# A layer of attention and experts on one core: the order of the prologue, of the routing steps and of the last product

## The reference

```python
x = L0_attn_h                                   # (2, 1024, 256)
xn = _layernorm(x)
x = x + attn(xn) + ffn(xn)

def attn(h):                                    # 16 heads of 128
    z = layernorm(h) * ln_g + ln_b
    q, k, v = z @ wq.T + bq, z @ wk.T + bk, z @ wv.T + bv
    q, k = rope(q), rope(k)
    a = softmax(causal(q @ k.T / sqrt(128)))
    return (a @ v) @ wo.T + bo + h

def ffn(x):                                     # 2048 tokens, 32 experts
    scores = sigmoid(x @ gate_w.T)              # + bias; best 2 of 4 groups, then best 4 experts
    out = moe(x, topk_idx, topk_w * 2)          # at most 64 rows per expert, in token order
    shared = silu(x @ shared_gate) * (x @ shared_up) @ shared_down
    return out + shared
```

## Time and profile before

| | |
|---|---|
| time, median of 3 runs | 1031.75 us (1031.66 to 1031.94) |
| time of the profiled execution | 1031.76 us |
| span of the profiled execution, first to last instruction | 1029.5 us |
| busy: TensorE, VectorE, GpSimd, ScalarE | 1014.0, 717.4, 768.8, 664.8 us |
| chain that ended last: TensorE, VectorE, GpSimd | 91%, 4%, 2% |
| granted clock of TensorE, mean | 0.997 |
| granted clock from about 10.3 to 13.7 us | 0.53 in that stretch, behind an idle TensorE from 7.06 to 8.87 us |
| TensorE busy in 0 to 25, 25 to 50, 50 to 75, 75 to 100 us | 20.64, 24.39, 23.06, 23.54 us |
| TensorE busy in 1000 to 1029.5 us | 25.34 us |

### The profile page before, as it was taken

One profiled execution on the slowest core, in us unless ns is written; L12 is line 12 of the kernel. 1 busy time (PEld: TensorE's weight loads), 2 busy tenths in 40 slices (PEclk: granted clock), 3 DMA queues, 4 the chain that ended last, 5 costly groups with the idle time before them and its releaser, 6 DMA issues.

```text
span 1029.5 us, 18761 instructions
## 1 busy us (share of the span) xinstructions
PE 1014.0 (98%) x6461; PEld 906.7 (88%) x6461; DVE 717.4 (70%) x1746; ACT 664.8 (65%) x1454; POOL 768.8 (75%) x656
## 2 busy tenths in 40 slices
PE   8999999999999999999999999999999999999998
PEld 4788898899988898899989999899998989898997
DVE  8966777787787778766566666666666575665676
...
DMA packets 51677, 75.42 MB, mean 73 GB/s; under 512 B 12288, under 2 KB 29056, under 8 KB 51456
## 3 DMA queue, kind: packets, MB, share of 16 engines
...
...
## 4 chain that ended last, share of the span: by engine, by line
PE 91%; DVE 4%; POOL 2%; ACT 1%; DMA 1%; issue 0%; SPq 0%; DVEq 0%; POOLq 0%; ACTq 0%
PE ps L302 25%; PE ps L304 25%; PE ps L303 25%; PE ps L441 12%; PE ps L524 3%; PE ps L536 1%; DVE ps L1541 1%; POOL qb L1686 1%; POOL qb L1682 1%; POOL qs L1683 1%; DMA qs<-qb 0%; DMA ra_<-sh_gate 0%; ACT prob L1038 0%; DVE st L1232 0%; PE ps L510 0%
## 5 line engine op out<-in xcount | busy, mean ns | idle before, releaser
L1682 POOL TENSOR_TENSOR qb<-qb,k_sb 128x512 f32<-128x512 f32 x128 | 171.7, 1341 | 148.3 <-DMA qs<-qb 148.0
L1541 DVE CUSTOM_DVE_ANT_0 ps<-ps,maskr 128x128 f32<-128x128 f32 (+7 forms) x256 | 193.8, 762 | 58.3 <-PE ps L304 58.0
L1038 ACT ACTIVATE prob<-ps,nmax 128x128 f32<-128x128 f32 (+7 forms) x256 | 190.5, 744 | 61.6 <-DVE nmax L1541 59.8
L1049 ACT ACTIVATE ptd_h<-ps 128x128 fp32r<-128x128 f32 (+3 forms) x256 | 109.4, 436 | 152.2 <-PE ps L441 151.2
L1551 DVE TENSOR_TENSOR ptd_l<-ps,ptd_h 128x128 fp32r<-128x128 f32 (+3 forms) x256 | 124.4, 486 | 83.6 <-ACT ptd_h L1049 81.5
L1686 POOL TENSOR_TENSOR qb<-qb,qs 128x512 f32<-128x512 f32 x128 | 165.8, 1296 | 18.7 <-POOL qs L1683 0.4
L441 PE MATMUL ps<-k_sb,prob 128*128 128x128 f32 x1152 | 172.8, 274 | 3.4 <-DVE ol L1564 1.5
L1683 POOL TENSOR_TENSOR qs<-qs,k_sb 128x512 f32<-128x512 f32 x128 | 173.7, 1357 | 0.0
L441 PEld LDWEIGHTS ps<-k_sb,prob 128*128 128x128 f32 x1152 | 135.4, 141 | 20.6 <-issue 3.4
L302 PE MATMUL ps<-k_h,q_h 128*128 128x512 f32 (+3 forms) x384 | 140.2, 365 | 0.6 <-ACT ztmp L920 0.5
L1581 DVE SCALAR_TENSOR_TENSOR acc<-ps,rinv,acc 128x256 f32<-128x256 f32 x256 | 111.6, 478 | 32.5 <-PE ps L304 30.9
...
## 6 DMA issues: line engine op xcount, KB each, us to landing
qs<-qb SPq DMA_DIRECT2D x256, 128.0 KB, 2.3
...
```

The costliest lines, as they stand in the source:

```text
L1038: act.activation(prob[:, t % 2, 0:w], tile[t], ACT.Exp, bias=nmax[:, t:t + 1], scale=-1.0, accum_out=rsum[:, t:t + 1]).then_inc(exp_done, 1)
L1049: act.activation(turned(0, t, j0, w), src, ACT.Copy).then_inc(pth_done, 1)
L1541: dve.tensor_tensor_reduce(out=tile[t], in0=tile[t], in1=maskr[:, SEQ - w:SEQ], scale=-1.0, scalar=3e38, op0=ALU.add, op1=ALU.min, accum_o ...
L1682: pool.tensor_tensor(qb[:, i, :], qb[:, i, :], cos_sb[:, c], ALU.mult).then_inc(rope_a, 1)
```

## The change

The change moves instructions; it adds no arithmetic, apart from one VectorE operation and one DMA at the end. Its parts:

1. Prologue, first rows: `shared_lo_w(0)` and `shared_lo_w(1)` go from VectorE to GpSimd, each behind a `root_of` of group 0. On VectorE x_lo(0) stands ahead of first_root(1) and stats(1,0), stats(1,1) behind z_lo(0) and wqk_lo(0), stats(2,0) behind x_lo(1,0). On ScalarE both x_hi stand ahead of shared_w(1); wv_hi, shared_w(2) and wo_hi behind logits(0); shared_tanh(0,0) directly behind again(0). On TensorE shared(0,0,0) stands ahead of z's turns, with 17 and 8 dummies instead of 12 and 13, and shared(0,1,1) ahead of project(0,0).
2. Prologue, later: values(0,1) ahead of turn_x(2,1), values(0,2) ahead of down(1,0), down(3,0) ahead of scores(0,0).
3. Units: in unit 0 project(1,2) ahead of turn(0,2); masks(9,1) behind weighted and exps, masks(9,3) behind scores(9,7).
4. Routing: the pieces are dealt anew over units 9 to 12, and the DMA of the weights is waited for in unit 12, not 11.
5. End: the last `out_lo_part`, outproj, add_out and the output DMA are halved.

The diff, cut to what the text speaks of:

```diff
             pe.wait_ge(zeros_ready, 1)
-            idle(12)
+            idle(17)
             pe.wait_ge(id_in, 16)
             turn_tiles(xn, "xt", xn_tile, xn_ready)
-            idle(13)
+            idle(8)
+            shared(0, 0, 0)
             turn_tiles(zz, "zt", z_tile, z_ready)
             gate(0)
-            shared(0, 0, 0)
             shared(0, 0, 1)
             shared(0, 1, 0)
             turn_x(1, 0)
+            shared(0, 1, 1)
             project(0, 0)
-            shared(0, 1, 1)
             project(0, 1)
...
             shared(1, 0, 1)
+            values(0, 1)
             turn_x(2, 1)
             down(0, 0)
             shared(1, 1, 1)
-            values(0, 1)
...
             gate_turn(1)
+            values(0, 2)
             down(1, 0)
-            values(0, 2)
...
             gate_turn(3)
+            down(3, 0)
             scores(0, 0)
-            down(3, 0)
             down(3, 1)
...
                 scores(n, 3)
+                weighted(n - 1, 1, range(4))
                 masks(n, 1)
-                weighted(n - 1, 1, range(4))
+                if n == 0:
+                    project(n + 1, 2)
                 turn(n, 2)
                 weighted(n - 1, 1, range(4, 8))
                 expert_turn(n)
                 scores(n, 4)
-                project(n + 1, 2)
+                if n:
+                    project(n + 1, 2)
...
                 scores(n, 6)
-                masks(n, 3)
...
                 scores(n, 7)
+                masks(n, 3)
...
             shared_w(0)
             x_hi(0, 0)
+            x_hi(0, 1)
             shared_w(1)
-            wv_hi(act, 0)
-            x_hi(0, 1)
             gate_w()
             again(0)
+            shared_tanh(0, 0)
             affine(0, 0)
             affine(0, 1)
-            shared_w(2)
-            wqk_hi(act, 0)
-            wo_hi(act, 0)
             z_hi(0, 0)
             z_hi(0, 1)
-            shared_tanh(0, 0)
+            wqk_hi(act, 0)
             logits(0)
+            wv_hi(act, 0)
+            shared_w(2)
+            wo_hi(act, 0)
...
             stats(0, 0)
-            shared_lo_w(dve, 0)
             first_root(0)
             norm(0)
             stats(0, 1)
-            stats(1, 0)
-            first_root(1)
-            shared_lo_w(dve, 1)
             x_lo(0, 0)
             x_lo(0, 1)
+            first_root(1)
+            stats(1, 0)
             gate_w()
             biases_q()
+            shared_g(0, 0)
             norm(1)
+            z_lo(dve, 0, 0)
+            z_lo(dve, 0, 1)
+            wqk_lo(dve, 0)
             stats(1, 1)
...
+                elif n == MASKS and at == 1:
+                    route_chosen_scores()
                 elif n == MASKS and at == 2:
+                    route_scan(0)
+                elif n == MASKS + 1 and at == 0:
+                    route_scan(1)
+                elif n == MASKS + 1 and at == 1:
+                    route_want()
+                elif n == MASKS + 1 and at == 2:
                     route_sums()
-                elif n == MASKS + 1 and at == 1:
+                elif n == MASKS + 2 and at == 0:
+                    route_find(0)
+                elif n == MASKS + 2 and at == 1:
                     route_inverse()
-                elif n == MASKS + 1 and at == 2:
+                elif n == MASKS + 2 and at == 2:
                     route_weights()
-                elif n == MASKS + 1 and at == 0:
-                    route_scan(0)
-                elif n == MASKS + 2 and at == 0:
-                    route_scan(1)
-                elif n == MASKS + 2 and at == 2:
-                    route_find(0)
...
             root_of(0, 0, 1)
+            shared_lo_w(pool, 0)
             root_of(0, 1, 2)
+            shared_lo_w(pool, 1)
             root_of(1, 0, 3)
             wv_lo(pool, 0)
-            pool.wait_ge(swl_ready, 2)
             shared_lo_w(pool, 2)
```

More of the change, by code:

```diff
@@ L497, in outproj @@
                 for i in range(2):
+                    single = u == UNITS - 1 and c == i2 == 1
+                    if single:
+                        pe.wait_ge(ol_done, 2 * u + 3 + i)
+                        if i:
+                            bank = take("OQ", u)
                     t = slice((2 * i2 + i) * P, (2 * i2 + i + 1) * P)
@@ L816, in _ @@
             sp.dma_start(out_t[2], acc[:, 2 * GT:3 * GT, :]).then_inc(stored, 16)
-            for i in range(2):
-                sp.wait_ge(add_done, 4 * (UNITS - 1) + 3 + i)
-                t = slice(3 * GT + 2 * i, 3 * GT + 2 * i + 2)
-                sp.dma_start(out_t[3, :, 2 * i:2 * i + 2, :], acc[:, t, :]).then_inc(stored, 16)
-            sp.wait_ge(stored, 16 * 5)
+            for done, a, b in ((3, 0, 2), (4, 2, 3), (5, 3, 4)):
+                sp.wait_ge(add_done, 4 * (UNITS - 1) + done)
+                sp.dma_start(out_t[3, :, a:b, :], acc[:, 3 * GT + a:3 * GT + b, :]).then_inc(stored, 16)
+            sp.wait_ge(stored, 16 * 6)
         def rope_in(act, m, i):
@@ L1304, in _ @@
             stats(0, 1)
-            stats(1, 0)
-            first_root(1)
-            shared_lo_w(dve, 1)
             x_lo(0, 0)
             x_lo(0, 1)
+            first_root(1)
+            stats(1, 0)
             gate_w()
             biases_q()
+            shared_g(0, 0)
             norm(1)
+            z_lo(dve, 0, 0)
+            z_lo(dve, 0, 1)
+            wqk_lo(dve, 0)
             stats(1, 1)
-            wqk_lo(dve, 0)
-            z_lo(dve, 0, 0)
-            shared_g(0, 0)
-            z_lo(dve, 0, 1)
-            stats(2, 0)
+            shared_u(0, 0)
             shared_g(0, 1)
             x_lo(1, 0)
-            shared_u(0, 0)
+            stats(2, 0)
             shared_u(0, 1)
+            x_lo(1, 1)
             norm(2)
-            x_lo(1, 1)
             stats(2, 1)
@@ L1452, in route_scan, with route_want @@
                                                ALU.add, ALU.add))
+            def route_want():
+                stepped(dve.tensor_scalar(want[:, :], k_sb[:, C_CV:C_CV + CG], 1.0, None, ALU.add))
             def route_find(half):
                 j = slice(half * CG // 2, (half + 1) * CG // 2)
-                if half == 0:
-                    stepped(dve.tensor_scalar(want[:, :], k_sb[:, C_CV:C_CV + CG], 1.0, None, ALU.add))
                 stepped(dve.max_index(found[:, j], want[:, j], cum))
@@ L1567, in out_lo_part @@
                 dve.wait_ge(oh_done, 2 * u + 2 + h)
-                o = slice(2 * h * P, (2 * h + 2) * P)
-                dve.tensor_tensor(ol[1][:, o], rbank("PW" if h else "PV", u, 1)[:, o], oh[1][:, o].bitcast(F32),
-                                  ALU.subtract).then_inc(ol_done, 1)
+                for o in (slice(2 * P, 3 * P), slice(3 * P, CH)) if h else (slice(0, 2 * P),):
+                    dve.tensor_tensor(ol[1][:, o], rbank("PW" if h else "PV", u, 1)[:, o], oh[1][:, o].bitcast(F32),
+                                      ALU.subtract).then_inc(ol_done, 1)
             def add_out(u, c, i2):
@@ L1578, in add_out @@
                 for i in range(2):
+                    bank = rbank("OP", u, c, i2)
+                    if single and i:
+                        dve.wait_ge(op_done, 4 * u + 5)
+                        bank = rbank("OQ", u)
                     j = 4 * c + 2 * i2 + i
                     t = batch_of(u) * TILES + j
-                    ins = dve.scalar_tensor_tensor(out=acc[:, t, :], in0=rbank("OP", u, c, i2)[:, i * DM:(i + 1) * DM],
+                    ins = dve.scalar_tensor_tensor(out=acc[:, t, :], in0=bank[:, i * DM:(i + 1) * DM],
                                                    scalar=rinv[:, j:j + 1], in1=acc[:, t, :], op0=ALU.mult, op1=ALU.add)
-                ins.then_inc(add_done, 1)
+                    if i or single:
+                        ins.then_inc(add_done, 1)
             def expert_copy(n):
```

13 lines of the change are left out of this document (8 added, 5 removed), and 2 rows, old and new, of the table pro_uses.

## The result

| | before | changed |
|---|---|---|
| time, median of 12 runs each | 1031.77 us (1031.18 to 1033.28) | 1034.64 us (1034.05 to 1036.66) |
| profiled execution: time, span | 1031.76, 1029.5 us | 1034.80, 1032.9 us |

The changed kernel takes 1.0026 of the time before (95% interval 1.0018 to 1.0034): 2.9 us longer. Forecast were 1036.8 us, in a range of 1028.5 to 1039.0, and slower by over 0.2% with 0.64. In the profiled executions the span grew by 3.4 us but the time by 3.0: what lies outside the span is 1.90 us now and was 2.26. Delays read from the traces are delays in the span.

A forecast was written before the change was run, and what follows sets the result against it. It took TensorE, busy 98% of the span, as the bound. Its terms, +8.4 through the prologue, -1.3 at 74 to 83 us, -1.7 in units 9 to 12 and -0.4 at the end, gave +5.0: 1036.8 us, range 1028.5 to 1039.0.

The forecast's parts named there:

- The port: VectorE and GpSimd operations wait each other out: norm(0) begins at 8.9, first_root(1) is held to 14.85; the sum's largest input.
- `wqk_lo` held by `wv_lo` to 24.4: Prologue: wv_lo gets in ahead of wqk_lo with 1.3 us, to 24.4, so stats(1,1) end at 26.2.
- again(1) at 31.4, TensorE's wait 3.6: Prologue: again(1) ends at 31.4 instead of 26.93, and TensorE waits 3.6 us at turn_z(1,0).
- norm(2) 6.3 us: Prologue, VectorE: norm(2)'s four tiles take turns with four GpSimd rope operations, 32.65 to 38.9; project(0,2) then +10.0.
- Given back up to 54 us: Values products cover TensorE's stalls at 39.35 and 52.08, -2.0; turn_z(2,0) waits 0.4 to 0.9; down(1,0) is +8.4.
- 74 to 83 us: down(3,0) ahead of scores(0,0) and project(1,2) as cover shorten TensorE's idle rows: -1.3 us.
- Units 9 to 12: Moved masks and redealt routing remove TensorE waits, less a scan's new wait: -1.7 us, between -2.9 and -1.0.
- The end: Halved last pieces release TensorE and start the first add earlier: -0.4 us, between -0.8 and +0.2.
- (a): Port holds but norm(2) isn't broken into turns: project(0,2) +4.2, time 1031.0; chance 0.12, shared with another rival.
- (c): Neither small operations nor norm(2) wait: project(0,2) +0.5 to +1.5, time 1027.3; chance 0.18.
- (b): Early operations slip past GpSimd's, norm(2) still meets the rotation: project(0,2) +6.3, time 1032.5 to 1033.8; chance 0.10.
- (d): TensorE's waits bring half-speed clock to the products behind 42.9, losing 1.7: 1038.5 us; chance 0.15.

The follow-up runs named there:

- e4: Changed kernel with GpSimd's rotation rope(0,0) made to wait until VectorE's norm(2) is done; 1033.47 us.
- e3: Changed kernel with VectorE's statistics moved back: stats(1,0) ahead of x_lo and first_root(1), stats(1,1) directly behind norm(1); 1033.62 us.
- e8: e3 with project(0,0) ahead of shared(0,1,1) on TensorE and ScalarE's copies wv_hi(0) and shared_w(2) early; 1031.56 us.
- e9: Changed kernel with only ScalarE's two copies wv_hi(0) and shared_w(2) early; 1037.04 us.
- b1: e1 with the routing's running sum in quarters and again(2) ahead of the mask copies on ScalarE; 1027.24 us.
- e7: e5 with project(0,0) ahead of shared(0,1,1) and shared_lo_w(0) and shared_lo_w(1) back on VectorE; 1034.50 us.
- e5: e3 with root_of(1,1) ahead of wv_lo(0) and shared_lo_w(2) on GpSimd; 1034.95 us.
- e1: Changed kernel with part 1 undone, parts 2 to 5 kept; 1028.31 us.

## Why the prediction was right, and where its steps were off

The sign and the mechanism of the waits were right; the time was 2.2 us too high, and one cause was missing. That the time lay in the range says little, as the range took in no change and a gain as well; the rows named beforehand say more. The error is a balance: 2.9 us too much at project(0,2), against 0.9 too much taken back at 74 to 83 us and smaller terms either way.

- **The port.** Right: norm(0) ended at 10.12 (10.28 by my sum), first_root(1) was held to 14.7 (14.85) and ended at 15.3 (15.5), norm(1) ended at 21.0 (21.25), norm(2) met the rotation. The sign named for it, a start at 8.9, did not come: norm(0) began at 7.69, as with free ports, and its wait of 1.05 us lies in its own four tiles (2.43), since the weight of `shared_lo_w(0)` landed later. In e4 the small operation ahead of it was held for 1.24 instead, and norm(0) ended at 10.36. The Trainium skill (SBUF — State Buffer, Who interferes with whom) has the shared ports as taken for a whole instruction; 13.39 and 13.45 agree, with one end for both.
- **`wqk_lo` held by `wv_lo` to 24.4.** Wrong: `wql` ended at 22.8 and GpSimd waited, so stats(1,1) were over at 24.53 and not at 26.2. Of these 1.7 us the root, begun at 25.27, lost 0.7 again, as I had no term for `wv_lo` and `shared_lo_w(2)` on GpSimd's own queue: 21.89 to 25.2, ahead of the root. The step that moved the two copies on ScalarE was costed by its wait for one operation, not by what stood behind it on GpSimd. In e3, with the statistics early, it is what holds the root. e8, with the statistics and the copies early and project(0,0) ahead, gets back 3.1 of the 6.3 us of part 1; neither move alone does (e3, e9).
- **again(1) at 31.4, TensorE's wait 3.6.** 30.5 and 2.37.
- **norm(2) 6.3 us.** The mis-sized term: 4.69. Each tile did wait out one operation of GpSimd, as I had it, but a turn cost 1.3 to 1.5 us and not 1.65: a tile ended 0.15 behind GpSimd's operation, and my sum added its whole 0.35. And of the first operation only 0.53 was left, not 1.0. norm(2) also began 1.1 earlier. With z_lo of 1.94 that puts **project(0,2) at +7.1 and not +10.0**, all of the error of the sum and a little more.
- **Given back up to 54 us.** -1.4 (7.1 to 5.7); the sum had -1.6. The wait at turn_z(2,0) came, 0.81.
- **74 to 83 us.** -0.4, not -1.3: 0.49 and 1.01 went, but 0.37 and 0.39 came right behind, since project(1,2) now stands between the products and the copies that follow them.
- **Units 9 to 12.** -2.1 (5.6 to 3.5), with -1.7 in the sum. Unit 9 gave 0.2: 0.69 and 0.77 went, 0.79 and 0.59 came; the first is the scan's, by the rows above, and it went with the shorter scan in b1. Unit 11 gave 1.8.
- **The end.** About -0.1, not -0.4. TensorE's last product is 3.4 us later than before and the span 3.4 longer, so the halved sums and the smaller last DMA gained about as much as the additional DMA cost. Outside the span 0.4 us went that the sum had no term for. It is 1.8 to 1.9 us in the runs with the first two low parts on GpSimd and 2.2 to 2.3 in those with them on VectorE, e7 among these; why is open.
- **Rivals.** (a) and (c) fell with 4.69 at norm(2) and +7.1. (b) fell with the 1.25 us for which first_root(1) was held, though one of its three terms, the 1.3 of `wv_lo`, did drop out. (d): the clock fell to 1.2 GHz behind the wait of 2.37, but at 31 to 35 us and not behind project(0,2), where the next waits took it up, so it added nothing to speak of; in e4 the same fall cost 1.1 us, in e5 2.2. The Trainium skill (TensorE: Matmul & The Clock Gate, HAM oscillation) has waits between groups of products, there for DMAs, throttle the engine again. The tables by stretches agree, though not throughout: behind the wait of 2.97 in e3's trace the clock stayed at 1.00. What the fall costs hangs on what comes last in the slow stretch.

Open: of the 3.3 us between e8 and e1 no run tells the shares of stats(2,0) behind x_lo(1,0), of `shared_g(0,0)` ahead of norm(1), of x_lo ahead of first_root(1), of the low parts on GpSimd and of shared(0,0,0) ahead of z's turns. The trace of e8 points at the first two, with the late again(0) of the third behind the second.
